# The projections of the first attention, written out with four store buffers, with its fills and its second pass of loads moved

## The reference, cut to what matters

```python
x = L0_attn_x
x = x + _L0_attn_ref(_layernorm(x), Wq, bq, Wk, bk, Wv, bv, Wo, bo)
...
def _L0_attn_ref(x, Wq, bq, Wk, bk, Wv, bv, Wo, bo):
    q = x @ Wq + bq
    k = x @ Wk + bk
    v = x @ Wv + bv
    q, k, v = (split_heads(q), split_heads(k), split_heads(v))
    scores = einsum('bhqd,bhkd->bhqk', q, k) / sqrt(HEAD_DIM)
    scores = where(causal, scores, -10000.0)
    probs = softmax(scores)
    ctx = einsum('bhqk,bhkd->bhqd', probs, v)
    return ctx @ Wo + bo
```

## Time and profile before

| | us |
|---|---|
| median of 3 runs | 3328.3 |
| the profiled execution, its own time | 3324.21 |
| its span, first to last instruction | 3322.4 |
| setup | 0 to 24.3 |
| project0 | 24.3 to 111.6 |
| attention0 up to its first transposed score | 111.6 to 148.0 |

### The profile page before, as it was taken

One profiled execution on the slowest core, in us unless ns is written; L12 is line 12 of the kernel. 1 busy time (PEld: TensorE's weight loads), 2 busy tenths in 40 slices (PEclk: granted clock), 3 DMA queues, 4 the chain that ended last, 5 costly groups with the idle time before them and its releaser, 6 DMA issues. The chain is left out here.

```text
span 3322.4 us, 74089 instructions
## 1 busy us (share of the span) xinstructions
PE 2573.5 (77%) x23657; PEld 1446.4 (44%) x23705; DVE 2685.7 (81%) x8584; ACT 2384.4 (72%) x3987; POOL 2024.4 (61%) x4543
## 2 busy tenths in 40 slices
PE   3599999759647777777777777775777777749999
PEld 2233333234424455455454544443454445544444
DVE  5788888334759999999999999998999999644444
ACT  2266666624249999999999999997999999712222
POOL 3133333420248899999999989996988999540000
PEclk8699999979866777777777777776777777868999
DMA  5312121000220101100110110110110010010000
GB/s 147 100 45 55 51 52 44 14 26 29 72 66 2 18 2 18 18 13 8 18 17 3 18 18 5 15 18 2 18 18 7 13 18 2 2 33 3 7 7 10
DMA packets 115268, 85.92 MB, mean 26 GB/s; under 512 B 58153, under 2 KB 97339, under 8 KB 114875
## 3 DMA queue, kind: packets, MB, share of 16 engines
q1 hardware_dynamic: 106331, 75.20, 10.4%
q0 software_dynamic: 8192, 4.79, 1.0%
q10 hardware_dynamic: 352, 1.18, 0.1%
HBM read 54.25 MB, written 19.40 MB: 22 GB/s over the span
## 5 line engine op out<-in xcount | busy, mean ns | idle before, releaser
L1462 POOL TENSOR_TENSOR a_near<-a_side,a_z 128x1024 int32<-128x1024 int32 x512 | 968.4, 1891 | 42.7
L1358 PE MATMUL a_ST<-a_qs,a_ks 75*128 75x128 bf16 x4096 | 661.4, 250 | 400.5 <-DVE a_mask L1595 208.8
L1558 DVE MAX8 a_cand<-a_near 128x8 f32<-128x256 f32 x2048 | 810.7, 414 | 0.0
L1358 PEld LDWEIGHTS a_ST<-a_qs,a_ks 75*128 75x128 bf16 x4096 | 461.2, 114 | 574.2 <-DVE a_mask L1595 343.4
L1602 DVE TENSOR_SCALAR_CACHE_REDUCE a_z<-a_S,a_thr 128x1024 f32<-128x1024 f32 x512 | 649.8, 1269 | 14.3 <-POOL a_thr L1438 8.4
L1382 ACT ACTIVATE a_signs<-a_z,a_tiny 128x1024 bf16<-128x1024 f32 x512 | 589.5, 1151 | 74.5 <-DVE a_z L1602 72.1
L1375 ACT ACTIVATE a_signs<-a_S,search 128x1024 bf16<-128x1024 f32 x512 | 571.7, 1117 | 5.3 <-PE a_S L1313 5.2
L1397 ACT ACTIVATE a_eT<-a_ST 128x1024 f32<-128x1024 f32 x512 | 519.9, 1015 | 18.8 <-PE a_ST L1359 18.4
L971 ACT ACTIVATE a_eT<-a_ST 128x512 f32<-128x512 f32 (+3 forms) x768 | 329.2, 489 | 210.4 <-PE a_ST L956 154.9
L1313 PE MATMUL a_S<-a_ks,a_qs 72*128 72x512 bf16 x1024 | 392.6, 472 | 82.9 <-DVE a_z L1602 76.8
L1075 DVE TENSOR_REDUCE a_mx<-a_S 128x1 f32<-128x512 f32 (+3 forms) x768 | 381.6, 547 | 77.9 <-PE a_S L943 68.1
(11 more groups left out here) (362 smaller groups left out, 4420.0 us busy)
## 6 DMA issues: line engine op xcount, KB each, us to landing
a_qs<-q_parts SPq DMA_DIRECT2D x174, 64.0 KB
a_ks<-k_parts SPq DMA_DIRECT2D x174, 64.0 KB
a_qs<-a_flip SPq DMA_DIRECT2D x512, 0.8 KB
q_parts<-p_qp SPq DMA_DIRECT2D x48, 128.0 KB, 2.0
k_parts<-p_kp SPq DMA_DIRECT2D x48, 128.0 KB, 2.0
a_qs<-q_parts SPq DMA_DIRECT2D x60, 96.0 KB
a_ks<-k_parts SPq DMA_DIRECT2D x60, 96.0 KB
f_w<-L_ffn_W SPq DMA_DIRECT2D x16, 256.0 KB, 2.9
```

The lines of the kernel that those rows point to most:

```text
L1358: pe.matmul(ST[:, block_of], ks[:, base(hl) + kb * P:base(hl) + (kb + 1) * P], qs[:, tile(hl):tile(hl) + P], start=True, stop=False)
L1462: pool.tensor_tensor(near[:, hl % NEARS, :].bitcast(I32), side[:, one].bitcast(I32).broadcast_to([P, SEQ]), z[:, hl % H, :].bitcast(I32), ...
L1558: mm = dve.max(found[:, 8 * g:8 * g + 8], near[:, h2 % NEARS, g * SW:(g + 1) * SW])
```

## The change

- `setup`: `arrange` comes after the aggregation of mean and variance instead of ahead of the last piece of x. The square root (ScalarE) and its reciprocal (VectorE) move from project0 into setup.
- `project0` is written out on all engines. q parts, k parts and v have four buffers (`HELD`), each with its own `stored` semaphore; the float32 intermediates and the PSUM tiles have two, xT's now as well. The cast of q's residue moves from VectorE to ScalarE. VectorE normalises two chunks ahead; TensorE turns the next chunk between a chunk's keys and values; q and k each release ScalarE by themselves.
- ScalarE issues no transfers. SP issues fill 0, stores 0 and 1, fill 1, store 2, the loads of pass 0, stores 3 to 7, fill 2.
- The loads of pass 1, and fill 3, are issued inside attention0: pass 1 right behind the first load of v, fill 3 behind `store_max(0)`.

```diff
-                ln0 = [front.enter_context(nc.sbuf_tensor(f"ln0_{x}", [P, NT], F32)) for x in ("mean", "var")]
+                ln0 = [front.enter_context(nc.sbuf_tensor(f"ln0_{x}", [P, NT], F32)) for x in ("mean", "rstd")]
                 k.fill = [front.enter_context(nc.sbuf_tensor(f"fill_{x}", [P, 2 * SEQ], BF16)) for x in ("zero", "one")]
                 setup(nc, k, inp, ln0)
                 k.qs, k.ks = (front.enter_context(nc.sbuf_tensor(f"a0_{x}", [P, 4 * G0 * SEQ], BF16)) for x in ("qs", "ks"))
                 k.kq_in = [front.enter_context(nc.semaphore(f"a0_kq_in{c}")) for c in range(2)]
+                k.blank_s = [front.enter_context(nc.semaphore(f"a0_blank{x}")) for x in range(4)]
                 project0(nc, k, ln0)
...
+        var_s, std_s = sem("su_var_done"), sem("su_std_done")
+        var, std = (ctx.enter_context(nc.sbuf_tensor(x, [P, NT], F32)) for x in ("su_var", "su_std"))
...
+        @block.scalar
+        def _(act):
+            act.wait_ge(var_s, 1)
+            act.activation(std[:, :], var[:, :], ACT.Sqrt).then_inc(std_s, 1)
+
...
                 dve.wait_ge(x_in[b], 16)
                 for t in range(b * IB, (b + 1) * IB):
                     dve.bn_stats(bn[:, t, :], k.x[:, t, :])
-                if b == 2:
-                    dve.wait_ge(loaded, 16 * len(loads))
-                    arrange()
             dve.drain()
             for t in range(NT):
                 dve.bn_aggr(mv[:, t, :], bn[:, t, :])
             dve.drain()
+            dve.tensor_scalar(var[:, :], mv[:, :, 1], LN_EPS, None, ALU.add).then_inc(var_s, 1)
             dve.tensor_copy(ln0[0][:, :], mv[:, :, 0])
-            dve.tensor_scalar(ln0[1][:, :], mv[:, :, 1], LN_EPS, None, ALU.add)
+            dve.wait_ge(loaded, 16 * len(loads))
+            arrange()
+            dve.wait_ge(std_s, 1)
+            dve.reciprocal(ln0[1][:, :], std[:, :])
...
+    HELD = 4
+    STORES = 16 * (2 * SPLIT + 1)
...
+        qp, kp = four(sb, "qp", [D, SPLIT, CW], BF16), four(sb, "kp", [D, SPLIT, CW], BF16)
+        vst = four(sb, "vst", [P, CT, D])
+        xT_ps, q_ps, k_ps, v_ps = (pair(ps, x, [P, CW]) for x in ("xT_ps", "q_ps", "k_ps", "v_ps"))
...
+            def normalize(n):
+                if n >= 2:
+                    dve.wait_ge(turned, n - 1)
+                for t in range(n * CT, (n + 1) * CT):
+                    dve.tensor_scalar(xn[n % 2][:, t % CT, :], k.x[:, t, :], mean[:, t:t + 1], rstd[:, t:t + 1],
+                                      ALU.subtract, ALU.mult).then_inc(xn_s, 1)
+
+            def residue(n):
+                dve.wait_ge(q_s, n + 1)
+                if n >= 2:
+                    dve.wait_ge(cast_s, n - 1)
+                dve.tensor_tensor(qres[n % 2][:, :], qf[n % 2][:, :], qp[n % HELD][:, 0, :], ALU.subtract).then_inc(qres_s, 1)
+
+            def add_bias_v(n):
+                bias = k.bv_all[0][:, :].rearrange("p (o d) -> p o d", o=1).broadcast_to([P, CT, D])
+                if n >= HELD:
+                    dve.wait_ge(stored[n % HELD], STORES * (n // HELD))
+                dve.wait_ge(v_done, n + 1)
+                dve.tensor_tensor(vst[n % HELD][:, :, :], v_ps[n % 2][:, :].rearrange("p (t d) -> p t d", t=CT), bias, ALU.add).then_inc(v_s, 1)
+
+            def last_part(n):
+                dve.wait_ge(cast_s, n + 1)
+                dve.tensor_tensor(qp[n % HELD][:, 2, :], qres[n % 2][:, :], qp[n % HELD][:, 1, :], ALU.subtract).then_inc(qlast_s, 1)
+
+            normalize(0)
+            normalize(1)
+            for n in range(NCH):
+                residue(n)
+                if n + 2 < NCH:
+                    normalize(n + 2)
+                add_bias_v(n)
+                last_part(n)
 
...
-            project_chunks(0)
-            project_chunks(1)
-            for c in range(CB):
-                act.wait_ge(stored[c], free(1))
-            act.wait_ge(blank_s[0], 64)
-            load_pass0(act, k, 0)
-            project_chunks(2)
-            project_chunks(3)
...
+            def take_queries(n):
+                act.wait_ge(q_done, n + 1)
+                if n >= 2:
+                    act.wait_ge(qres_s, n - 1)
+                if n >= HELD:
+                    act.wait_ge(stored[n % HELD], STORES * (n // HELD))
+                act.activation(qf[n % 2][:, :], q_ps[n % 2][:, :], ACT.Identity, bias=k.bq[0][:, 0:1])
+                act.activation(qp[n % HELD][:, 0, :], q_ps[n % 2][:, :], ACT.Identity, bias=k.bq[0][:, 0:1]).then_inc(q_s, 1)
+
+            def take_keys(n):
+                act.wait_ge(k_done, n + 1)
+                if n >= 2:
+                    act.wait_ge(ksplit, SPLIT * (n - 1))
+                act.activation(kf[n % 2][:, :], k_ps[n % 2][:, :], ACT.Identity, bias=k.bk[0][:, 0:1])
+                act.activation(kp[n % HELD][:, 0, :], k_ps[n % 2][:, :], ACT.Identity, bias=k.bk[0][:, 0:1]).then_inc(k_s, 1)
+
+            def cast_residue(n):
+                act.wait_ge(qres_s, n + 1)
+                if n >= 2:
+                    act.wait_ge(qlast_s, n - 1)
+                act.activation(qp[n % HELD][:, 1, :], qres[n % 2][:, :], ACT.Copy).then_inc(cast_s, 1)
+
+            copy_turned(0)
+            for n in range(NCH):
+                take_queries(n)
+                if n + 1 < NCH:
+                    copy_turned(n + 1)
+                take_keys(n)
+                cast_residue(n)
 
...
+            turn(0)
+            for n in range(NCH):
+                products(n)
+                if n + 1 < NCH:
+                    turn(n + 1)
+                values(n)
 
...
-            fill(0)
-            store(0)
-            fill(1)
-            store(1)
-            fill(2)
-            store(2)
-            fill(3)
-            store(3)
-            sp.wait_ge(blank_s[1], 64)
-            load_pass0(sp, k, 1)
-            sp.wait_ge(blank_s[2], 64)
-            sp.wait_ge(blank_s[3], 64)
...
+            def store(n):
+                b, c = n // CB, n % CB
+                cols, held = slice(c * CW, (c + 1) * CW), n % HELD
+                sp.wait_ge(qlast_s, n + 1)
+                for s in range(SPLIT):
+                    sp.dma_start(k.q_parts[s, b * D:(b + 1) * D, cols], qp[held][:, s, :]).then_inc(stored[held], 16)
+                sp.wait_ge(v_s, n + 1)
+                sp.dma_start(k.v_rows[0][n * CW:(n + 1) * CW, :].rearrange("(t p) d -> p t d", p=P), vst[held][:, :, :]).then_inc(stored[held], 16)
+                sp.wait_ge(ksplit, SPLIT * n + SPLIT)
+                for s in range(SPLIT):
+                    sp.dma_start(k.k_parts[s, b * D:(b + 1) * D, cols], kp[held][:, s, :]).then_inc(stored[held], 16)
+
+            fill_pass0(sp, k, 0)
+            for n in range(CB):
+                store(n)
+            fill_pass0(sp, k, 1)
+            store(CB)
+            for n in range(CB):
+                sp.wait_ge(stored[n], STORES)
+            sp.wait_ge(k.blank_s[0], 64)
+            load_pass0(sp, k, 0)
+            for n in range(CB + 1, NCH):
+                store(n)
+            fill_pass0(sp, k, 2)
+            for held in range(HELD):
+                sp.wait_ge(stored[held], STORES * NCH // HELD)
+
+
+def fill_pass0(queue, k, x):
+    for rows, odd in ((slice(64, P), 0), (slice(0, 64), 1)):
+        cols = slice((2 * x + odd) * 2 * SEQ, (2 * x + odd + 1) * 2 * SEQ)
+        for dst, const in ((k.qs, k.fill[0]), (k.ks, k.fill[1])):
+            queue.dma_start(dst[rows, cols], const[rows, :]).then_inc(k.blank_s[x], 16)
 
 
...
             load_v(0)
+            sp.wait_ge(k.blank_s[1], 64)
+            load_pass0(sp, k, 1)
             sp.wait_ge(kq_in[0], 16 * DMAS_Q)
+            sp.wait_ge(k.blank_s[2], 64)
             load_pass0(sp, k, 2)
             store_max(0)
+            fill_pass0(sp, k, 3)
+            sp.wait_ge(k.blank_s[3], 64)
             for it in range(ITERS):
...
```

160 lines of the change are left out of this document (43 added, 117 removed).

## The result

The changed kernel takes 3308.2 us (median of 4 runs, 3305.0 to 3309.3) beside 3327.9 us (3326.6 to 3328.9) for the kernel before: ratio 0.9939, 95% interval 0.9922 to 0.9957, so 14 to 26 us faster. The forecast was 3305 and 23 us. The profiled execution took 3308.9 us, 15.3 us less than that of before.

A forecast was written before the change was run, and what follows sets the result against it. Transfers in SP's one queue were taken to end project0: attention0 starts 26.5 us earlier, less a 3.6 us wait for maxima, 22.9 us; 3328.3 - 23 = 3305 us (chance 0.50), range 3293 to 3317.

The forecast's parts named there:

- The setup: Setup and project0's start: setup ends at 20.8, 3.5 us earlier; first normalised tile at 21.0, a gain of 5.5 us.
- The compute pace: Project0: VectorE and GpSimd counted as one line of work, 5.8 us a chunk becoming 5.4; chunk 7's keys at 71.9.
- That the transfers bind: Project0: eight stores (27.2), fill 1 (4.85), pass 0 (16.5) and some 2 us idle end at 82.6, after the compute's 71.9.
- The end of project0: Transfers through at 82.6, then landing and the engines' meeting: attention0 starts at 85.1, against 111.6 before.
- the landing and the meeting of engines: End of project0: from the transfers' end at 82.6 to attention0's start at 85.1, with 1.8 to 2.1 us for landing.
- The first rival: Project0: transfers keep up, compute pace ends the stage, attention0 starts at 76.6; gain 30.4, 3298 us; chance 0.22.
- Store 3 must land before chunk 7's queries, at about 67 to 70, and does: Late project0: with four buffers store 3 lands in time, so chunk 7 does not wait; with two, chunk 5 would.
- The rival of the stall: Project0: chunk 7 waits for store 3 behind pass 0 as chunk 4 did; gain some 12 us, 3317 us; chance 0.09.
- Pass 1 just in time: Opening of attention0: pass 1, loaded inside, lands at 108.3 and is needed at 108.4; no cost taken.
- The wait for the maxima: Attention0's first transposed score: row maxima, stored behind pass 2, land at 125.1 but are wanted at 121.5; 3.6 us wait.
- Fill 3 and pass 3 behind that ...; zero: Attention0: fill 3 and pass 3, queued behind the maxima, arrive some 20 us before first use; cost zero.
- The sum: First transposed score at 125.1 instead of 148.0: 22.9 us gained, 26.5 from the earlier start less 3.6 of wait.

## Why the prediction was right, and where its steps failed

**The setup** was right: stage end 20.7 for 20.8, first tile 20.77 for 21.0; alone it is worth 5.3 us for 5.5.

**The compute pace** was forecast at 5.4 us. (The 5.8 us of before are the mean of the first four starts, 34.20 to 51.63; the two that the forecast names lie 5.9 apart.) With eight buffers, where nothing is late, it is 5.2 at the mean (bias of v from 29.35 to 65.74 in seven steps), but the steps go from 2.8 to 8.6 us. In the changed kernel VectorE's normalise of four tiles took 4.63 us from 32.97, while GpSimd's operations ran back to back from 32.6 to 37.5, and 1.10 us at 39.32, with GpSimd idle: VectorE does wait for GpSimd. The mean did not touch the result, since the compute ended at 70.7 with enough buffers (forecast 71.9) and the stage at 87.4; the slow step from chunk 0 to chunk 1 did, as told below.

**That the transfers bind** was right in its size. From 42.25 to 84.5, SP issued fill 1, pass 0 and six stores; the forecast's prices for these are 4.85 + 16.5 + 6 x 3.4 = 41.8 us, and it took 42.2. A pass beside stores cost 14.4 us (forecast 16.5): 21.5 us from 52.29 to 73.82 with stores 3 and 4, less 7.1 for two stores at the pace of the last ones (3.57). But what binds has another name: not the engines of the transfers, but SP's issues, some lengthened by the backlog on a few engines. It shows in the unbroken run of issues up to 0.6 us before the start, and in the run with pass 1 and fill 3 back, where the start moved by just their issue time. The runs without fills (start 5.0 us earlier) and with pass 0 on ScalarE (SP's end 4.9 us earlier) fit it, though each also takes bytes from in front of the last stores. With pass 0 gone the start came only 1.7 us earlier, since the last chunk, a memset and landings then set the end. The Trainium skill ("DMA: Bandwidth & Descriptors", "Issuing engines are not separate DMA queues") says that a second issuing engine saves issue time only. The last of these runs agrees in that SP's end came earlier by 4.9 us; whether transfer time was saved as well no run here shows.

**The end of project0** was forecast at 85.1 and came at 88.4. Two steps failed. "Some 2 us in which the first chunks leave it idle" were 3.4, because of chunk 1 (fill 1 begins at 42.25, not 40.8). And "the landing and the meeting of engines", 2.5 us behind the last store, left out that SP must first issue fill 2: 84.5 to 87.8, so 3.9 us. The first rival had counted that issue; the forecast's own sum had not.

**"Store 3 must land before chunk 7's queries, at about 67 to 70, and does"** was wrong: ScalarE waited 14.15 us for it, since store 3 is issued behind all of pass 0, and its last three issues took 4.50 us. The sentence did not fit the forecast's own line: 32.0, four stores (13.6), fill 1, pass 0 and the 2 us of idle time put store 3 through at 69.0 and landed at about 71. And the queries were ready earlier than taken, at 60.4 (74.56 - 14.15), where the forecast has 67 to 70. The forecast lists "a store's landing stops VectorE for 10 us" as a sign of being wrong; that sign came (14.2 us), and the time did not follow. The rival of the stall (3317 us) had this event and the wrong price: it assumed that a stall at chunk 7 costs what it cost at chunk 4. The forecast had also misread the stall of before: VectorE went on at 72.64 when store 2 had landed, not store 3. Eight buffers remove the stall of the changed kernel and gain 1 us or nothing. A chunk that waits at the end of the list, while SP has a backlog of stores that are ready, cost next to nothing here. At chunk 5, with two buffers, the same kind of wait cost 8.8 us.

**Pass 1 just in time** was right; no wait for it shows. **The wait for the maxima** was forecast at 3.6 us and is 6.2. The backlog of pass 2 was sized well: with fill 3 held back the wait is 3.5. The failing step is "Fill 3 and pass 3 behind that ...; zero": the fill is issued right behind the maxima, and takes 2.7 us from them.

**The sum.** 22.9 us at the first transposed score, measured 17.4: 3.3 lost at project0's end, 2.6 at the maxima, less 0.4 that TensorE idled at that place before as well. From there to the last copy next to nothing is lost (505.1 and 505.5 us). The median moved by 19.7 us, more than this mark; that the time lies only 3.2 us from the forecast while the mark lies 5.5 from it is luck of the scatter, as the interval of 14 to 26 us allows. By single parts, 5.3 come from the setup and 6.0 to 8.9 from moving pass 1 and fill 3; what is left, 3 to 6 us, is the rewritten projections with pass 0 on SP, four buffers and all. Four buffers are worth 8.8 us against two, so by this account, which takes the parts to add up, the rest of that rewriting costs 3 to 6 us and only the buffers turn it into a gain. The rewriting alone, the new order of a chunk's stores and pass 0 on SP were not tried by themselves in the kernel before.

## What to carry over

Before pricing a stall, look at what the last finisher of the stage was doing meanwhile: if the queue that ends the stage had ready work all along, the stall costs next to nothing (14 us of waiting, 1 us at most), and if the queue ran dry, about the time for which it was dry (19 us of waiting, 9.4 us dry, 8.8 us lost). Count the time to issue transfers as work of its own engine, and put into the sum everything that still stands in that queue when the last needed transfer is in, such as a fill for later. In this kernel a small transfer that someone waited for was delayed by large ones issued ahead of it on few engines, and also by those issued right behind it.

## What the runs showed of the hardware

- The issue of a load on SP takes 0.29 to 0.54 us for a copy of 8 rows and 0.61 to 0.82 us for those of 16 and 24 rows, where nothing holds it up. A pass of 36 copies took 12.3 us in the steady part and 13.5 and 14.8 in project0; one of 16 took 10.4. The three key stores take 1.3 to 1.6 us in a quiet queue and 4.50 behind a pass on few engines. In the version with copies of 8 rows the stores behind the pass kept their 1.5 us.
- GpSimd's memset of 128x4096 bf16 takes 3.51 us. VectorE's takes 3.47 us for ones but 1.76 us for zeros, which the profile shows as 2048 uint32. Beside GpSimd's memset VectorE's statistics of the inputs kept their pace (1.65 us for eight), but an operation on 128x32 took 2.68 us, to the end of the memset, where it takes 0.18 alone.
- The middle of the program, attention1, differs by up to 6 us between profiled executions of kernels that are alike in it (2143 to 2149 us from project1's first transposition to the first product of the last expert block). Gains of 2 us in the first stages are seen in the marks but not in the time.
